# A routed expert kernel: three subtractions moved to GpSimd, counting of experts 2 to 7 moved ahead, x tiles cut by halves of the contraction

## What is computed

```
rot    = rotated x                                    # linear in x
probs  = softmax(rot @ gate_w.T)                      # 4096 x 8
assign = the fewest experts, largest first, whose probabilities reach 0.9
key    = probability - rank, for assigned pairs
keep   = for each expert the 512 tokens with the largest keys
y      = sum over kept experts of prob * gelu(rot @ w1[e].T) @ w2[e].T
out    = x + y
```

## Time and profile before

| | |
|---|---|
| median of 3 runs | 265.87 us |
| profiled execution | 266.03 us |
| its span, first to last instruction | 264.2 us |
[...]
| PE busy | 92% |
| DVE busy | 75% |
| ACT busy | 57% |
| POOL busy | 52% |
| chain that ended last | PE 64%, DVE 16%, DMA 11% |

### The profile page before, as it was taken

One profiled execution on the slowest core, in us unless ns is written; L12 is line 12 of the kernel. 1 busy time (PEld: TensorE's weight loads), 2 busy tenths in 40 slices (PEclk: granted clock), 3 DMA queues, 4 the chain that ended last, 5 costly groups with the idle time before them and its releaser, 6 DMA issues.

```text
span 264.2 us, 4054 instructions
## 1 busy us (share of the span) xinstructions
PE 244.1 (92%) x1450; PEld 184.6 (70%) x1450; DVE 199.5 (75%) x439; ACT 149.6 (57%) x276; POOL 136.8 (52%) x105
## 2 busy tenths in 40 slices
PE   8887878788999999999999999999999999999970
PEld 2455432236997788887888888888788888888750
DVE  5387899997799997977997798789779966933220
ACT  4721058851657758746865774687377658734100
POOL 1000000047743787687578749756875781487530
PEclk9999999999999999999999999999999999999996
DMA  6999999977973498589559856973994690372521
GB/s 245 423 415 410 501 330 317 329 248 238 345 248 98 56 279 221 122 177 277 146 71 261 234 99 125 294 189 45 236 236 127 87 226 6 42 84 43 180 90 40
DMA packets 12771, 53.78 MB, mean 204 GB/s; under 512 B 2752, under 2 KB 3136, under 8 KB 9536
## 3 DMA queue, kind: packets, MB, share of 16 engines
q1 hardware_dynamic: 4496, 35.68, 37.8%
q0 software_dynamic: 8256, 17.85, 32.8%
HBM read 44.74 MB, written 18.22 MB: 238 GB/s over the span
## 4 chain that ended last, share of the span: by engine, by line
PE 64%; DVE 16%; DMA 11%; issue 2%; POOL 2%; ACT 1%; SPq 0%; POOLq 0%; DVEq 0%
PE bank L852 10%; PE bank L867 10%; PE bank L854 10%; PE bank L853 10%; PE bank L868 10%; PE bank L872 10%; DMA region<-in_xt 7%; DVE region L702 4%; PE bank L833 4%; DVE w1rot L513 3%; DMA w1raw<-in_w 3%; DMA xg<-in_x,gath 1%; POOL xg L300 1%; PE bank L925 1%; ACT w1rot L354 1%
## 5 line engine op out<-in xcount | busy, mean ns | idle before, releaser
L316 POOL DMA_INDIRECT out<-ysb,scat x32 | 63.4, 1980 | 42.8 <-ACT ysb L395 31.8
L513 DVE SCALAR_TENSOR_TENSOR w1rot<-w1raw,rot,w1rot 128x512 f32<-128x512 f32 x84 | 63.1, 752 | 6.7 <-ACT w1rot L354 4.7
L852 PE MATMUL bank<-w2h,hh 128*128 128x512 f32 x128 | 51.5, 402 | 0.1
L854 PE MATMUL bank<-w2h,hl 128*128 128x512 f32 x128 | 50.1, 391 | 0.0
L853 PE MATMUL bank<-w2l,hh 128*128 128x512 f32 x128 | 50.0, 391 | 0.0
L300 POOL DMA_INDIRECT xg<-in_x,gath x16 | 17.0, 1062 | 62.1 <-DVE gath L566 57.8
L867 PE MATMUL bank<-xh,w1h 128*128 128x512 f32 x112 | 44.0, 393 | 0.0
L868 PE MATMUL bank<-xh,w1l 128*128 128x512 f32 x112 | 43.6, 390 | 0.0
L544 DVE TENSOR_TENSOR hl<-hf,hh 128x512 fp32r<-128x512 f32 x32 | 22.0, 688 | 26.1 <-ACT hh L386 26.1
L382 ACT ACTIVATE hf<-bank 128x512 f32<-128x512 f32 x32 | 19.1, 596 | 35.9 <-PE bank L872 32.9
L308 POOL DMA_INDIRECT score<-probs_scratch,pidx x32 | 34.0, 1061 | 9.7 <-issue 9.4
(11 more groups left out here) (144 smaller groups left out, 370.4 us busy)
## 6 DMA issues: line engine op xcount, KB each, us to landing
region<-in_xt SPq DMA_DIRECT2D x8, 1024.0 KB, 9.6
w1raw<-in_w SPq DMA_DIRECT2D x8, 1024.0 KB, 11.6
w2raw<-in_w SPq DMA_DIRECT2D x8, 1024.0 KB, 8.0
score<-probs_scratch,pidx POOLq DMA_INDIRECT x32, 5.8
out<-ysb,scat POOLq DMA_INDIRECT x32, 5.9
probs_scratch<-probs SPq DMA_DIRECT2D x1, 384.0 KB, 28.4
ch<-in_ch SPq DMA_DIRECT2D x1, 320.5 KB, 10.5
xg<-in_x,gath POOLq DMA_INDIRECT x16, 3.7
```

What stands on the lines that cost most here:

```text
L316: pool.indirect_dma_start(out_d, bass.IndirectOffsetOnAxis(scat[:, e, s:s + 1], 0), ysb[:, s, :], None, compute_op=ALU.add if e < LAST els ...
L513: ins = nc.vector.scalar_tensor_tensor(dst, w1raw[:, e % 2, i, :], rot[:, j, i:i + 1], dst, ALU.mult, ALU.add)
L852: nc.tensor.matmul(dst, ah, bh, start=first, stop=False)
L854: return nc.tensor.matmul(dst, al, bh, start=False, stop=last)
```

## The change

1. The tiles of x are cut otherwise. Before, a tile was 512 tokens by all 512 features; now it is 1024 tokens by 256 features, also 1 MB. `gate(c, h)` is 8 matmuls of 256 columns. The two halves of a chunk add up in one bank, so there is one evacuation of 256 columns for a chunk and two transposes behind it. ScalarE makes its diagonals after exp instead of before the evacuations. The small table `cf` is loaded behind tile 1.
2. `lev` of a chunk is made in two halves of 544 columns; the second stands behind the centring of the next chunk.
3. GpSimd makes the low parts of blocks 0, 1, 2 of expert 0's w1, each as soon as its high part is there, ahead of the gathers in its program. VectorE keeps block 3.
4. VectorE counts the tokens of experts 2 to 7 right behind the slot tables of expert 1, ahead of the low parts of x; TensorE's `count_before` for them stands ahead of the first transposes of x, instead of between layer 1's first and second part; ScalarE evacuates it before the first gelu.

The diff, without some index changes that follow from it:

```diff
-            sp.dma_start(cf[:, :], cf_d).then_inc(cf_in, 16)
             load_x(1)
+            sp.dma_start(cf[:, :], cf_d).then_inc(cf_in, 16)
...
+            for j in range(C4 - 1):
+                pool.wait_ge(w1_hi, j + 1)
+                nc.gpsimd.tensor_tensor(w1l[0][:, j, :], w1rot[:, j, :], w1h[0][:, j, :].bitcast(FP32),
+                                        ALU.subtract).then_inc(w1_lo, 1)
             gather_x(0)
...
-            def part_out(g):
-                act.wait_ge(parts_mm, g + 1)
-                if g >= 2:
-                    act.wait_ge(logits_mm, g - 1)
-                nc.scalar.activation(parts[:, g % 2, :], pbank[g % 2][:, 0:P], ACT.Copy).then_inc(parts_ev, 1)
+            def part_out(c):
+                act.wait_ge(parts_mm, 2 * (c + 1))
+                if c >= 2:
+                    act.wait_ge(logits_mm, c - 1)
+                nc.scalar.activation(parts[:, c % 2, :], pbank[c % 2][:, 0:2 * P], ACT.Copy).then_inc(parts_ev, 1)
...
             x_high0(0)
             x_high0(1)
+            rows_out(1, 2, E)
             for e in range(E):
...
-                    rows_out(1, 2, E)
...
+            def key_levels(c, h):
+
+                ts = slice(h * TPG, (h + 1) * TPG)
+                nc.vector.tensor_tensor(lev[c % 2][:, ts].rearrange("p t (l e) -> p t l e", e=E),
+                                        cav("levels").rearrange("p (l e) -> p l e", e=E).unsqueeze(1).to_broadcast([P, TPG, TL, E]),
+                                        key16[:, ts, :].unsqueeze(2).to_broadcast([P, TPG, TL, E]), ALU.is_gt).then_inc(lev_ready, 1)
...
                 order_keys(c)
+                key_levels(c, 0)
                 if c + 1 < len(CHUNKS):
                     centre(c + 1)
+                key_levels(c, 1)
                 close_keys(c)
+                dve.wait_ge(lev_ready, 2 * (c + 1))
...
-            w1_low(0, 0, 1)
             dve.wait_ge(tb_mm, 1)
...
             rows_of_slots(0, 0, S4 // 2)
-            w1_low(0, 1, 2)
             slot_tables(0)
             slots_after(1)
-            w1_low(0, 2, 3)
+            w1_low(0, 3, C4)
             slot_tables(1)
-            w1_low(0, 3, C4)
+            count_tokens(2, E)
             x_low0(0)
             x_low0(1)
-            count_tokens(2, E)
             w2_low(0)
...
-                for j in range(C4):
+                for j in range(C4 // 2):
                     for u in range(TPG):
-                        last = nc.tensor.matmul(pbank[g % 2][u * GW:(u + 1) * GW, 0:P], gfold[:, j, :],
-                                                xt[:, g % XRING, j, u * P:(u + 1) * P], start=(j == 0), stop=(j == C4 - 1))
+                        last = nc.tensor.matmul(pbank[c % 2][u * GW:(u + 1) * GW, 0:2 * P], gfold[:, h * C4 // 2 + j, :],
+                                                xt[:, g % XRING, j, u * 2 * P:(u + 1) * 2 * P],
+                                                start=(h == 0 and j == 0), stop=(h == 1 and j == C4 // 2 - 1))
...
             keep_clock(8, cbank[1])
+            count_before(1, 2, E)
             transpose_x0(0)
...
                     transpose_x0(3)
-                    count_before(1, 2, E)
                     layer1_half(1)
```

More of the change, by code:

```diff
@@ L135, in build @@
         region = sb("region", [P, XRING * C4 * TG])
[L136 removed]
+        xt = region[:, :].rearrange("p (r c n) -> p r c n", r=XRING, c=C4 // 2)
         probs = sb("probs", [P, NT, ZW])
@@ L194, in build @@
                xg[0][:, 2:4, :].rearrange("p s d -> p (s d)").bitcast(FP16)[:, 0:TPG * 2 * NL].rearrange("p (t l) -> p t l", l=NL)]
-        parts = hf[:, :, 0:P]
+        parts = hf[:, :, 0:2 * P]
         diag = ysb[:, :, :].rearrange("p s d -> p (s d)").rearrange("p (q c) -> p q c", c=P)
@@ L263, in _ @@
             load_x(0)
+            load_x(1)
             sp.dma_start(cf[:, :], cf_d).then_inc(cf_in, 16)
-            load_x(1)
             sp.dma_start(ca[:, :], ca_d).then_inc(ca_in, 16)
@@ L433, in rows_out @@
                     nc.scalar.activation(begin[:, e0:e1], starts_of(n, e0, e1), ACT.Copy).then_inc(begin_ready, 1)
-            g = 0
-            for c, (_, hi) in enumerate(CHUNKS):
-                while g < hi // TPG:
-                    if g < C4:
-                        diagonal(g)
-                    part_out(g)
-                    g += 1
+            for c in range(len(CHUNKS)):
+                part_out(c)
                 exp(c)
+                if c < 2:
+                    diagonal(2 * c)
+                    diagonal(2 * c + 1)
             for r in range(ROUNDS):
@@ L916, in layer2, with gate, logits_by_token @@
                 last.then_inc(y_mm, 1)
-            def gate(g):
+            def gate(c, h):
+                g = 2 * c + h
                 pe.wait_ge(xt_in[g % XRING], 16 * (g // XRING + 1))
-                if g >= 2:
-                    pe.wait_ge(parts_ev, g - 1)
-                for j in range(C4):
+                if c >= 2 and h == 0:
+                    pe.wait_ge(parts_ev, c - 1)
+                for j in range(C4 // 2):
                     for u in range(TPG):
-                        last = nc.tensor.matmul(pbank[g % 2][u * GW:(u + 1) * GW, 0:P], gfold[:, j, :],
-                                                xt[:, g % XRING, j, u * P:(u + 1) * P], start=(j == 0), stop=(j == C4 - 1))
+                        last = nc.tensor.matmul(pbank[c % 2][u * GW:(u + 1) * GW, 0:2 * P], gfold[:, h * C4 // 2 + j, :],
+                                                xt[:, g % XRING, j, u * 2 * P:(u + 1) * 2 * P],
+                                                start=(h == 0 and j == 0), stop=(h == 1 and j == C4 // 2 - 1))
                 last.then_inc(parts_mm, 1)
-            def logits_by_token(g):
-                c = g // 2
-                if c >= 2 and g % 2 == 0:
+            def logits_by_token(c):
+                if c >= 2:
                     pe.wait_ge(centred, c - 1)
-                pe.wait_ge(parts_ev, g + 1)
-                at = g % 2 * P
-                nc.tensor.transpose(lbank[c % 2][:, at:at + P], parts[:, g % 2, :], ident).then_inc(logits_mm, 1)
+                pe.wait_ge(parts_ev, c + 1)
+                for v in range(2):
+                    vs = slice(v * P, (v + 1) * P)
+                    last = nc.tensor.transpose(lbank[c % 2][:, vs], parts[:, c % 2, vs], ident)
+                last.then_inc(logits_mm, 1)
             def count_ahead(c):
@@ L945, in count_levels @@
             def count_levels(c):
-                pe.wait_ge(lev_ready, c + 1)
                 for t in range(TPG * 2):
+                    if t % TPG == 0:
+                        pe.wait_ge(lev_ready, 2 * c + 1 + t // TPG)
                     last = nc.tensor.matmul(nbank[:, 0:NL], cav("ones"), lev[c % 2][:, t, :],
@@ L969, in _ @@
             for c in range(len(CHUNKS)):
-                gate(2 * c)
+                gate(c, 0)
                 if c == 0:
-                    pe.wait_ge(cf_in, 16)
+                    keep_clock(3, kbank, blank)
                 if c >= 2:
                     count_levels(c - 2)
-                else:
-                    keep_clock(2, kbank, blank)
-                logits_by_token(2 * c)
                 if c == 1:
@@ L981, in _ @@
                     count_ahead(c - 1)
-                else:
-                    keep_clock(2, kbank, blank)
-                gate(2 * c + 1)
+                gate(c, 1)
+                if c == 0:
+                    pe.wait_ge(cf_in, 16)
                 keep_clock(2, kbank, blank)
-                logits_by_token(2 * c + 1)
+                logits_by_token(c)
             count_levels(2)
@@ L1116 @@
     rows = np.concatenate([np.asarray(x).reshape(N, D), np.zeros((P, D), np.float32)])
-    xt = np.ascontiguousarray(rows[0:N].reshape(P, NG, TPG, C4, P).transpose(1, 4, 3, 2, 0)).reshape(NG, P, C4, TG)
+    xt = np.ascontiguousarray(rows[0:N].reshape(P, NG // 2, 2, TPG, 2, C4 // 2, P).transpose(1, 4, 6, 5, 3, 2, 0))
+    xt = xt.reshape(NG, P, C4 // 2, 2 * TG)
     cond, right = np.asarray(cond_256).T, np.asarray(L0_cond_q_right).T
```

7 lines of the change are left out of this document (1 added, 6 removed).

## The result

The changed kernel takes 269.6 us (four runs, 269.18 to 270.4) where the kernel before takes 265.8 (four runs on the same chip, 265.54 to 266.5). The ratio is 1.0124, with a 95% interval of 1.009 to 1.0158; that is 3.3 us, where the two medians differ by 3.8. Every ratio in this document leaves out runs over 1.5% above the fastest of their kernel. The forecast was 265.9, range 264.9 to 267.5: wrong, on the slow side. The profiled execution took 269.18 us for a span of 267.4, against 266.03 and 264.2 before: 3.2 us more.

The account below looks back on a forecast made before the run. The prediction took x-tile arrivals to bound the opening and expert 1's w1 load and rotation to hold TensorE until 87.32 us, then matmuls. Terms -0.45 + 0.2 + 0.25 = 0.0 gave 265.9 us, range 264.9 to 267.5.

Parts of the forecast that it names:

- Search: From 35 us to the first gathers at 56: GpSimd's three subtractions cost VectorE time, +0.2 us.
- Bounds 0 and 1.2: Limits in us set on the delay that GpSimd's subtractions cause VectorE in the search; value taken +0.2.
- rival 3: Search: VectorE's edge or thresholds wait out GpSimd's subtraction; once 266.9 us, three times 269.3; chance 0.20, slower.
- three waits are left out: Range 264.9 to 267.5 covered one or two VectorE waits in the search, not three (3.6 us, 269.3).
- the two can't read together: Search: condition under which a VectorE operation with two SBUF tensors waits out GpSimd's subtraction, 1.3 us less 0.1.
- the first gather's 1.30 us: Issue time beside a VectorE subtraction, against 0.96 for the second gather; read as hinting at 0.3 us mutual delay.
- may have begun: Search, argument against rival 3: two of the three pairs are closer still, so VectorE may have started before GpSimd.
- Opening: From 0 to 35 us: earlier tile 5, wider gate steps and split level halves, together -0.45 us.
- The packet: Opening: instruction packet at 17.8 delays tile 5; moved to 19.4 to 27 us, it lets tile 5 land 1.4 earlier.
- Gathers to layer 2: First gathers to 87.32 us: counting experts 2 to 7 ahead of the transposes costs +0.25, ends 0 and +0.7.
- The new wait: TensorE before the first transpose, behind the count of experts 2 to 7: 1.55 us on everything queued behind it.
- TensorE's slack against the rotation of w1: Before 87.32 us: TensorE has 0.79 us of slack, which leaves +0.27 of a +1.06 delay.

Follow-up runs that it names:

- experiment 1: Changed kernel with the three low parts of expert 0's w1 given back to VectorE: ratio 1.0065 to the kernel before, search 21.4 us.
- experiment 2: Kernel before with only the three subtractions moved to GpSimd: ratio 1.0118 to the kernel before, search 24.5 us.
- experiment 3: Changed kernel with GpSimd writing zeros instead of subtracting, at the same places: ratio 0.9986 to the kernel before, search 21.4 us.
- experiment 5: Changed kernel with GpSimd copying one tensor instead of subtracting, at the same places: ratio 1.0062 to the kernel before, search 22.5 us.
- experiment 4: Changed kernel with each GpSimd subtraction waiting until VectorE is past the operation it would meet: ratios 1.0024 and 1.0016 to the kernel before.
- experiment 12: Kernel before with two late subtractions on GpSimd, behind thresholds 4 and 6: ratios 1.0072, then 0.9979 (0.9957 to 1.0001) to the kernel before.
- experiment 10: Kernel before, with VectorE's block 2 subtraction and GpSimd's block 1 subtraction both right behind the search, block 0 late on GpSimd: one run, search 22.0 us.
- experiment 6: Kernel before with only the count of experts 2 to 7 moved ahead of layer 1: ratio 1.0046 to the kernel before, median 269.86 us.

## Why the prediction was wrong

**Search, +0.2 predicted, +3.08 measured: the step that failed.** The prediction put "Bounds 0 and 1.2; I take +0.2". Both the value and the upper bound were wrong, and for one reason: the bound was one wait, though three places were named. The mechanism stood in rival 3, with its price ("Three times: 3.6, 269.3") and a chance of 0.20, and "three waits are left out" of the range. It came true at 3 x 1.04. Experiments 1 and 2 show that the longer search comes from these three operations and from nothing else of the change, 3 and 5 that it takes a GpSimd operation that reads (the threshold 0.23 us beside the write, 0.62 beside the copy), 4 and 12 that it is gone when they don't meet (0.23). The 1.3 us for GpSimd's subtraction stood on no row of before, which has only VectorE's 0.68; three of them measured 1.26. That "the two can't read together" was an assumption too; what the changed kernel shows is thresholds of 1.29 us and an edge of 1.21 beside subtractions of 1.26.

Three things in the reasoning led there. The value rested on the first gather's 1.30 us beside a VectorE subtraction: a small delay of another kind of operation, taken as the nearest row for a meeting that no row showed (in the changed kernel the first gather takes 1.13 us with no subtraction beside it and the second 0.95, so only half of that 0.3 was mutual delay). The lengths of the two engines' operations were not compared: when the long one (1.26) is in front, the short one (0.23) pays nearly all of it. And the argument against, that VectorE "may have begun" where the gap was closer, holds only for a clear lead: 0.22 us was enough in experiment 10, 0.02 was not. Rival 3's own price, 1.2 a meeting, was a little high for 1.04. Rival 3's condition, GpSimd starting within 0.15 us of the rounding, was met: 42.09 to 42.18. Its argument that VectorE follows ScalarE in less than 0.15 us has a case in the kernel before: exp starts at 28.45 and takes 0.26 us, and the sum that waits for it starts at 28.80, 0.09 us behind its end, the same as GpSimd's.

**Opening, -0.45 predicted, -0.06 measured.** The packet moved as inferred: it lay at 17.8 to 18.0 and lies at 19.6 to 19.8, and tile 5's gate no longer waits for DMA. Gates of tiles 5, 6 and 7, and the packet from 19.6 to 19.8, in the changed kernel:

```profile
19.08 0.87 PE L949 MATMUL bank<-xg,ca 128*128 128x64 f16 x7 [0.72 <-DVE xg L645]
19.88 1.07 PE L931 MATMUL bank<-region,gfold 128*32 128x256 f32 x16
...
23.25 1.07 PE L931 MATMUL bank<-region,gfold 128*32 128x256 f32 x16 [1.30 <-DMA region<-in_xt]
25.79 1.07 PE L931 MATMUL bank<-region,gfold 128*32 128x256 f32 x16 [0.16 <-DMA region<-in_xt]
```

```profile
q8 instruction: 1, 0.02, 34.6%
```

Two pieces were missed. Tile 5's gate stands behind a count (L949) that waits for VectorE's mask, so it starts at 19.88, not 19.2; the prediction saw this for the last gate and not for this one. And tile 7 landed at 25.75, not 25.3, so its gate waits for it and the last centring starts at 27.90, where it started at 27.93 (27.45 predicted). The queues were full either way (97.9% of 16 engines in the packet's 0.2 us before, 98.2% after), and tile 6 is waited for until 23.25 instead of 23.09; that the packet passed its delay on to it is my inference.

What the prediction inferred, that the packet makes the tile behind it late, gets support from other profiles with the old opening. In the second profile of the kernel before the packet lies at 15.6 to 15.8, in experiment 10 at 15.4 to 15.6; there tile 4 is the late one (18.34 and 18.24 instead of 16.65) and tile 5's gate doesn't wait. So the packet's place isn't fixed by the program alone: it moved by 2.2 us between two executions of the same kernel.

**Gathers to layer 2, +0.25 predicted, +0.16 measured: right.** The new wait is there, with the releaser that was named, and the transposes behind it:

```profile
65.04 0.19 PE L1029 MATMUL bank<-incl,ch 128*128 128x12 f16 x1 [1.75 <-DVE incl L587]
...
65.59 0.60 PE L846 MATMUL bank<-cf,xg 128*128 128x128 f32 x4
```

From the first gather table to the first transpose it is 6.90 us instead of 5.48: +1.42, predicted 1.55. As worked out, 0.49 comes back where the count stood, and most of the rest went into TensorE's slack against the rotation of w1. What the prediction did not say is that this small price hangs on the GpSimd subtractions: with VectorE doing three low parts ahead of the count (experiments 1 and 6) the wait is 2.35 us, and in experiment 1 0.80 more arrives. Without the meetings the forecast would have held: by the traces -0.06 and +0.16 make +0.10, and experiment 3 measured 0.9986.

**Chances.** 0.34 stood on slower, 0.20 on the case that happened. Two inputs on one engine and a reading operation on the other stood at three named places within 0.15 us of each other; with that on the table, "three waits" deserved a place in the range.

## What to carry to other kernels

Work moved to GpSimd is not free because GpSimd is idle: before moving it, list what VectorE runs in the same microseconds, and look there for operations of the kinds that were held up here: with two SBUF tensors (threshold 1.29 instead of 0.23 us, edge 1.21 instead of 0.22, scan 0.74 and 1.02 instead of 0.42), or f16 ones like the four steps above (1.72 instead of 0.89). Price each at what is left of GpSimd's operation, as these were. The price is per meeting, so count meetings, and multiply before writing down a bound. What kept its time beside such work here were VectorE operations that read one tensor with an accumulator (0.48 us), or one of whose inputs is in PSUM (0.44). An operation that only writes cost nothing beside the threshold and the edge (0.23 and 0.22 us); beside the f16 steps it wasn't tried. And moving the work gained nothing even where it met nothing: experiment 12's interval reaches 1.

## What the runs showed of the hardware beyond that

GpSimd's times for 128x512 f32: 1.26 us to subtract two tensors, 0.61 to copy one, 0.53 to write zeros; VectorE subtracts in 0.68. GpSimd's tensor operation started 0.09 us after ScalarE's rounding ended (42.09 to 42.18), while 0.30 us of issue stood ahead of the second indirect gather. A stretch at half the granted clock came after TensorE had stood for 1.99 us in the opening or 3.65 us ahead of the counts, in experiment 2 after 0.94, but not in every execution with such waits (2.35 us in the profile of experiment 1, clock 1.00). And nine more filler matmuls ahead of the counts, which closed a wait of 2.35 us to 0.42, did not bring the time down: ten runs out of ten stood at 269.6 us or more, on a chip where the kernel before had a median of 267.2. I can't explain that.
